# A shared feed-forward stage by Strassen block products, with the second projection after the fifth product

## The reference

```python
s1 = xf @ shared_fc1.T          # 3584 x 512 by 512 x 1408
s2 = xf @ shared_fc2.T          # the same shape
shared = jax.nn.silu(s1) * s2 @ shared_proj.T      # 1408 -> 512
y = y + jax.nn.sigmoid(xf @ shared_gate_w.T) * shared
```

## Time and profile before

| | |
|---|---|
| median of the timed runs | 1615.07 us |
| the profiled execution, its own time | 1618.94 us |
| its span, first to last instruction | 1617.2 us |
| mean granted clock of TensorE | 0.99 |
| busy: PE, DVE, ACT, POOL | 97%, 54%, 39%, 35% |
| shared stage, first to last matmul | 1050.0 to 1609.7 us |
| busy in it: PE, DVE, ACT, POOL | 556.8, 185.8, 105.5, 56.3 us |

### The profile page before, as it was taken

The page is one execution under the profiler, slowest core; times in us unless marked ns, Lnnn a source line. Parts: engine busy times, 40 slices in busy tenths (PEclk is TensorE's granted clock), DMA queues, the critical chain, the costliest instruction groups (busy, mean ns, idle before and its releaser), DMA issues.

```text
span 1617.2 us, 32041 instructions
## 1 busy us (share of the span) xinstructions
PE 1563.1 (97%) x11388; PEld 1333.0 (82%) x11388; DVE 871.8 (54%) x1685; ACT 632.7 (39%) x1970; POOL 559.7 (35%) x507
## 2 busy tenths in 40 slices
PE   4999999999889999999999999999999999999998
PEld 3788888888768799999999999888788888888886
DVE  4567777766655576666666666544423233232322
ACT  3877777877743333332333333332111111121211
POOL 4233446445442355555555555220200100000010
PEclk9899999999999999999999999999999999999999
DMA  4233355443466366666566666454401203030110
GB/s 156 64 103 97 79 103 90 95 86 76 89 140 162 108 257 244 243 228 245 221 246 222 245 235 242 154 208 145 147 28 47 78 8 104 26 104 26 56 49 26
DMA packets 85684, 213.53 MB, mean 132 GB/s; under 512 B 38208, under 2 KB 39232, under 8 KB 80864
## 3 DMA queue, kind: packets, MB, share of 16 engines
q1 hardware_dynamic: 73424, 179.20, 35.3%
q0 software_dynamic: 12176, 33.20, 6.1%
HBM read 163.35 MB, written 49.02 MB: 131 GB/s over the span
## 4 chain that ended last, share of the span: by engine, by line
PE 86%; issue 4%; DVE 3%; POOL 3%; ACT 2%; DMA 2%; DVEq 0%; POOLq 0%; SPq 0%; ACTq 0%
PE psum L665 54%; PE psum L972 11%; PE psum L917 9%; PE psum L763 2%; PE psum L888 2%; PE psum L754 2%; PE psum L782 1%; ACT probs L1071 1%; PE psum L791 1%; PE psum L850 1%; PE psum L814 1%; POOL xn L1275 1%; PE psum L771 1%; PE psum L678 1%; POOL lists_dram L1241 1%
## 5 line engine op out<-in xcount | busy, mean ns | idle before, releaser
L665 PE MATMUL psum<-gT_hi,wj_hi 128*128 128x256 f32 (+1 forms) x840 | 238.9, 284 | 0.0
L665 PE MATMUL psum<-gT_lo,wj_hi 128*128 128x256 f32 (+1 forms) x840 | 236.4, 281 | 0.0
L665 PE MATMUL psum<-gT_hi,wj_lo 128*128 128x256 f32 (+1 forms) x840 | 235.7, 281 | 0.0
L1350 POOL DMA_INDIRECT routed<-expert_out_dram,slot_b x56 | 56.3, 1006 | 489.2 <-DVE slot_b L1737 336.5
L665 PE MATMUL psum<-nT_hi,ws_hi 128*128 128x512 f32 x528 | 209.8, 397 | 6.4 <-DVE nT_lo L1689 6.4
L1755 DVE TENSOR_TENSOR h_s<-psum,silu_s 128x512 f32<-128x512 f32 x66 | 45.6, 692 | 308.1 <-PE psum L665 308.1
L665 PE MATMUL psum<-nT_hi,ws_lo 128*128 128x512 f32 x528 | 211.0, 400 | 0.0
L665 PE MATMUL psum<-nT_lo,ws_hi 128*128 128x512 f32 x528 | 210.8, 399 | 0.0
L1312 POOL TENSOR_SCALAR wj_hi<-wj_raw 128x2816 fp32r<-128x2816 f32 x68 | 136.4, 2023 | 149.5 <-PE psum L917 123.2
L1071 ACT ACTIVATE probs<-psum,minus_max 112x112 f32<-112x112 f32 x512 | 176.3, 431 | 3.4 <-DVE minus_max L1437 3.4
L1679 DVE TENSOR_TENSOR wj_lo<-wj_raw,wj_hi 128x2816 fp32r<-128x2816 f32 x70 | 169.2, 2418 | 0.8 <-ACT wj_hi L1163 0.7
(11 more groups left out here) (219 smaller groups left out, 3581.8 us busy)
## 6 DMA issues: line engine op xcount, KB each, us to landing
wj_raw<-in_w_experts SPq DMA_DIRECT2D x35, 2176.0 KB, 8.6
expert_out_dram<-y_c SPq DMA_DIRECT2D x35, 512.0 KB, 2.7
wj_raw<-in_w_shared SPq DMA_DIRECT2D x22, 768.0 KB, 5.9
base<-x_dram SPq DMA_DIRECT2D x8, 1024.0 KB, 5.8
x_in<-in_x SPq DMA_DIRECT2D x32, 224.0 KB, 3.8
x_res<-in_x SPq DMA_DIRECT2D x32, 224.0 KB, 3.1
x_dram<-x SPq DMA_DIRECT2D x32, 224.0 KB, 2.8
normed_dram<-xn SPq DMA_DIRECT2D x32, 224.0 KB, 3.2
```

Source lines behind the costliest of these rows:

```text
L665: mm = pe.matmul(out_ap, u, v, start=(n == 0), stop=(n == last))
L1350: pool.indirect_dma_start(out=routed[:, b % 2, c, :], out_offset=None, in_=expert_out_dram, in_offset=bass.IndirectOffsetOnAxis(ap=slot_b[ ...
```

## The change

The 512 tokens of a group and the 512 input values are halved each, and so are pairs of chunks: a unit ("quads") is the first layer of two chunks for 512 tokens, as a product of 2 x 2 blocks. It is done with seven block products in place of eight (Strassen's scheme in Winograd's form). Each block product is 12 matmuls of 256 columns. Five units hold ten chunks; the eleventh ("one") stays as it was. The weights of a unit are loaded as four blocks, of which POOL makes seven (`sum_quads`, four additions or subtractions); a group's tokens are loaded as four blocks, and POOL makes four more (`sum_tokens`), so that there are eight, of which quads take seven. ACT and DVE split all of them into halves.

The halves of 5 units do not fit in SBUF. The stage now goes twice over the six groups: in the first run ("half 0") with units 0, 1, 2, in the second ("half 1") with unit 3, the single chunk, and unit 4. The first run stores its partial result back to `x1_dram`, the second adds to it. Weights of unit 3 and 4 are loaded, summed and split in the last group of the first run and the first of the second. Routed rows are added in the first run; those of the first 512 tokens in the second group of the second run.

What remains of a unit outside TensorE: the products land in banks 4 to 7, and DVE and ACT form the four result blocks (`m1`, `u2`, `u3`, `c22`, `c21`, `c12`) before SiLU, product and splitting. The two projections of a unit run in the unit behind it: one after its second product, the other after its fifth.

```diff
+        UNITS = ((("quads", 0, 0, (0, 1)), ("quads", 1, 1, (2, 3)), ("quads", 2, 2, (4, 5))),
+                 (("quads", 3, 0, (0, 1)), ("one", None, None, (6,)), ("quads", 4, 1, (2, 3))))
+        # weight block, token block, bank, fresh bank
+        PARTS = ((0, 0, 4, True), (5, 5, 5, True), (1, 2, 4, False), (2, 6, 6, True), (4, 4, 7, True), (3, 7, 5, True), (6, 3, 7, False))
...
 # PE
+            def part(half, g, i, q, n):
+                w, t, b, fresh = PARTS[n]
+                if i == 0 and n < 7:
+                    pe.wait_ge(S["t_split"], prepared_before(half, g) + PREPARED.index(t) + 1)
+                for f in range(2):
+                    for k in range(2):
...
+                        for m, (u, v) in enumerate(((a_hi, b_hi), (a_hi, b_lo), (a_lo, b_hi))):
+                            mm = pe.matmul(psum[:, b, f * HS:(f + 1) * HS], u, v, ...
+            def quads(half, g, i, q):
+                at_least(pe, S["sums_made"], summed(n - 1, "h11"))
+                part(half, g, i, q, 0)
+                at_least(pe, S["sums_made"], summed(n - 1, "c21"))
+                part(half, g, i, q, 1)
+                project_before(half, g, i, 0)
+                pe.wait_ge(S["copies_made"], copied(n, "m1"))
+                part(half, g, i, q, 2)
+                at_least(pe, S["sums_made"], summed(n - 1, "u3"))
+                part(half, g, i, q, 3)
+                at_least(pe, S["sums_made"], summed(n - 1, "c12"))
+                part(half, g, i, q, 4)
+                project_before(half, g, i, 1)
+                pe.wait_ge(S["sums_made"], summed(n, "u2"))
+                part(half, g, i, q, 5)
+                pe.wait_ge(S["sums_made"], summed(n, "c22"))
+                part(half, g, i, q, 6)
...
 # DVE, one unit
+                dve.tensor_tensor(m1[:, :, :], b5, m1[:, :, :], ALU.add).then_inc(S["sums_made"], 1)
...
+                if i == 2:
+                    low_behind(half, g, (0, 1))
+                    add_group(half, g, (1, 2))
...
+                dve.tensor_tensor(s1[:, 0, :], psum[:, 4, HS:ST], s1[:, 0, :], ALU.mult).then_inc(S["sums_made"], 1)
...
+                dve.tensor_tensor(u3[:, :, :], b6, m1[:, :, :], ALU.add).then_inc(S["sums_made"], 1)
+                if i == 2:
+                    low_behind(half, g, (2, 3))
+                if i == 1 and half == 0:
+                    place_group(half, g)
...
+                dve.tensor_tensor(c2[:, :, HS:ST], b7, u3[:, :, :], ALU.add).then_inc(S["sums_made"], 1)
+                before = unit_before(half, g, i) if i == 0 else None
+                if before:
+                    dve.wait_ge(S["proj_s_done"], chunks)
+                    for b in range(SB):
+                        add_shared(*before[0:2], b)
+                if i == 2:
+                    low_behind(half, g, (4,))
+                dve.wait_ge(S["part_done"], 7 * n + 6)
+                dve.tensor_tensor(c2[:, :, 0:HS], u3[:, :, :], b5, ALU.subtract).then_inc(S["sums_made"], 1)
+                dve.wait_ge(S["part_done"], 7 * n + 7)
+                dve.tensor_tensor(m1[:, :, :], b7, m1[:, :, :], ALU.add).then_inc(S["sums_made"], 1)
+                dve.wait_ge(S["copies_made"], copied(n, "c2"))
+                dve.tensor_tensor(c2[:, 0, :], c2[:, 0, :], c2[:, 1, :], ALU.mult).then_inc(S["sums_made"], 1)
+                dve.wait_ge(S["copies_made"], copied(n, "c12"))
+                dve.tensor_tensor(s1[:, 1, :], s1[:, 1, :], m1[:, 1, :], ALU.mult).then_inc(S["sums_made"], 1)
+                dve.wait_ge(S["hs_hi_made"], chunks + 1)
+                dve.tensor_tensor(hs_lo[:, 1, :], c2[:, 0, :], hs_hi[:, 1, :].bitcast(F32), ALU.subtract).then_inc(S["hs_split"], 1)
...
+                if i == 2:
+                    low_behind(half, g, (5, 6, 7))
+                    add_group(half, g, (3,))
+                if i == 1 - half:
+                    add_group(half, g, (0,))
...
 # POOL
+            def sum_quads(q):
+
+                w = quads_raw[UNITS_SLOT[q]]
+                pool.wait_ge(quads_loaded[q % 3], 64 * (q // 3 + 1))
+                for i, (to, a, b, op) in enumerate(((4, 2, 3, ALU.add), (5, 4, 0, ALU.subtract), (6, 1, 5, ALU.subtract), (2, 0, 2, ALU.subtract))):
...
+                    pool.tensor_tensor(w[:, to, :, :], w[:, a, :, :], w[:, b, :, :], op).then_inc(S["quads_summed"], 1)
...
+                if isinstance(n, int) and n == NJOBS - 2:
+                    sum_quads(0)
+                    sum_tokens(0, 1)
+                if last_job(n):
+                    sum_quads(1)
...
 # ACT, end of job 33
+                if isinstance(n, int) and n == NJOBS - 2:
+                    quads_high(0)
...
 # DVE, in the last job, behind chunk 0 and chunk 1
+                    elif i == 0:
+                        quads_low(0)
+                    else:
+                        for t in range(5):
+                            tokens_low(0, 1, t)
...
 # PE, at the very end
+            for j in range(SB):
+                y_of(1, 2, 0, j)
+                y_of(1, 2, 1, j).then_inc(S["y_block_done"], 1)
```

More of the change, by code:

```diff
@@ L108, in build_program @@
     WS = (2 * KC + 4) * P
+    HS = ST // 2
     ctx = ExitStack()
@@ new lines, in unit_before, with group_behind, quads_of @@
+        def unit_before(half, g, i):
+            if i:
+                return half, g, i - 1
+            if is_opening(g):
+                return (0, GB, 2) if half else None
+            return half, g - 1, 2
+        def group_behind(half, g):
+            return (1, 1) if is_turn(half, g) else (half, g + 1)
+        def quads_of(q):
+            return quads_hi[UNITS_SLOT[q]], quads_lo[UNITS_SLOT[q]]
+        UNITS_SLOT = (0, 1, 2, 0, 1)
+        PW_SEMS = (0, 1, 2, 0, 3, 1)
+        SUMS = ("u2", "h11", "u3", "c22", "c21", "c12", "h2", "h12")
@@ new lines, in chunk_of, with y_of @@
+            def chunk_of(half, i, n):
+                kind, _, _, places = UNITS[half][i]
+                return (1, places[0]) if kind == "one" else (1 - n, places[1 - n])
+            def y_of(half, i, n, j):
+                at, pw = chunk_of(half, i, n)
+                a_hi, a_lo = hs_hi[:, at, j * P:(j + 1) * P], hs_lo[:, at, j * P:(j + 1) * P]
+                last = i == 2 and n == 1
+                for m, (u, v) in enumerate(((a_hi, pw_hi[:, pw, :]), (a_hi, pw_lo[:, pw, :]), (a_lo, pw_hi[:, pw, :]))):
+                    mm = pe.matmul(bank(j), u, v, start=(i == 0 and n == 0 and m == 0), stop=(last and m == 2))
+                return mm
@@ L954, in hidden_s, with one @@
+            def one(half, g, i):
+                n = quads_before(half, g, i)
+                if is_opening(g):
+                    pe.wait_ge(S["one_split"], 1)
+                pe.wait_ge(S["t_split"], prepared_before(half, g) + 8)
+                for f, b in enumerate((4, 6)):
+                    pe.wait_ge(S["sums_made"], summed(n - 1, "u3" if f else "h11"))
                     pairs = []
                     for k in range(KC):
-                        cols = slice((c * KC + k) * P, (c * KC + k + 1) * P)
@@ new lines, in one @@
+            def one(half, g, i):
+                u = u3[:, :, :].rearrange("p f t -> p (f t)")
+                act.wait_ge(S["one_filled"], 2 * g - 1)
+                act.wait_ge(S["sums_made"], summed(quads_before(half, g, i) - 1, "c21"))
+                act.activation(u, bank(4), ACT.Silu).then_inc(S["one_silu"], 1)
+                act.wait_ge(S["one_made"], g)
+                act.wait_ge(S["proj_s_done"], chunks_before(half, g, i) - 1)
+                act.activation(hs_hi[:, 1, :], u, ACT.Copy).then_inc(S["hs_hi_made"], 1)
@@ L1188, in _, with shared_body @@
+            def shared_body(half, g):
+                for i, unit in enumerate(UNITS[half]):
+                    if unit[0] == "one":
+                        one(half, g, i)
+                    else:
+                        quads(half, g, i)
             act.wait_ge(S["phase_c_done"], 4)
@@ new lines, in add_routed, with place_group, add_group @@
+                    dve.wait_ge(S["routed_added"], 2 * (SB * n + b) + c + 1)
+            def place_group(half, g):
+                if half == 0:
+                    place_routed(g - 1, route_b, S["route_b_loaded"], 16 * base_turn(half, g))
+                elif isinstance(g, int) and g == 2:
+                    place_routed(GB, route_0, S["base_z_loaded"], 32)
+            def add_group(half, g, bs):
+                for b in bs:
+                    if half == 0:
+                        dve.wait_ge(S["base_loaded"], 16 * base_turn(half, g))
+                        add_routed(g - 1, b, base, route_b)
+                    elif isinstance(g, int) and g == 2:
+                        add_routed(GB, b, base_z, route_0)
```

547 lines of the change are left out of this document (378 added, 169 removed).

## The result

The changed kernel took 1628.43 us (median of five, 1625.90 to 1632.87) beside 1615.07 for the kernel before (five, 1613.65 to 1615.96): ratio 1.0091, interval [1.0076, 1.0106]. It is about 0.9% slower, as the forecast case said, but by 13 us and not by 3: inside the range of 1602 to 1632, above the 1611 to 1625 of the likeliest case. The profiled execution has a span of 1625.6 us, 8.4 more than before and 5.6 more than the sum of the prediction (1620). These two differences are too small by 3.1 us, for the changed kernel's execution was ahead when the changed part began.

A forecast was written before the change was run, and what follows sets the result against it. The prediction took PE issuing matmuls as the bound. Matmuls 515.9, waits 38.3, POOL 4 and clock 6 made 564 us; with start 1051.5 and tail 4.5 that is 1620, 1618 on the median's scale, range 1602 to 1632.

The forecast's parts named there:

- the forecast case: Whole kernel: the waits eat the gain, 3 us slower, 1611 to 1625 on the median's scale; chance 0.45.
- The gain: Shared stage: a unit's 84 matmuls at 0.119 us take 10.00 us against 11.22, saving 36.7 us over 30 units.
- wait of 0.3 us for `hs_lo` in each unit: Behind each unit's seventh product: chain of 3.07 us over a cover of 2.86, 0.31 us each, 9 us for 29 units.
- the first units: First unit of a group: adds of the group before delay the chain by 0.75 us; eleven such units, 8 us.
- the opening: Start of the shared stage: first unit waits 4.5 us for c22, the next about 2; 6.5 us together.
- POOL beside DVE in every group: POOL's sum_tokens stretch h2 and hs_lo by up to 1.3 us in eleven units, 0 to 14; 4 us taken.
- The clock: Opening, first unit, turn and end: four falls to 1.2 GHz of up to 1.9 us each; 6 us taken (2 to 9).
- The step that failed, opening: Job 34, ahead of the shared stage: it ends about 5 us later, so the stage starts at 1051.5 (1050 to 1053.5).
- The step that failed, turn: Third unit of group 6: late weights, then DVE work, put c22 at 49.5 to 50 against 47; 5 us (2 to 8).
- rival 4: The turn and the opening wait longer for weights, 8 us more, 1626; chance 0.07.
- Rival 3: POOL's sums fall on the chain in all groups, 14 us in place of 4, 1628; chance 0.12.
- rival 2: Shared stage: the waits are mostly covered, so the kernel is faster, 1603 on the median; chance 0.30.

The follow-up runs named there:

- the run of the turn alone: Changed kernel with GpSimd gathers, quads_hi, quads_lo and the block 2 add reordered in the third unit at the turn; ratio 1.0056 to the kernel before.
- the kernel with all of it together: Changed kernel with reordered opening and turn, adds of blocks 2 and 3 behind hs_lo, both projections early in each group's first unit; ratio 0.9932 to the kernel before.

## Why the prediction held and where it was off

**Right.** The gain: 256 columns at 0.119 us, so that the speed of the matmuls was never the question. The groups: 49.3 and 40.8 us forecast, 48.8 to 49.5 and 40.6 to 40.9 measured. The wait behind the first unit (1 us forecast; 0.54 to 0.80 and its restart), `c22` about 1 us late in the third (0.87 to 1.37 in groups 2 to 5), the end (3.8 and 3.6), the weights' landing at the turn 29 us into the group and their sums done at 35 (the group starts at 1305.3, since the projection at 1324.44 is 2.9 us into its second unit of 16.3; POOL sums from 1334.39 to 1340.3). The stage as a whole came out at 567.0 for 564, and the direction followed from the right cause, DVE's queue.

**Off by cancelling.** The "wait of 0.3 us for `hs_lo` in each unit" is there, and smaller. Where no other work is in the way, PE starts the projection 0.05 to 0.13 us late and its second matmul 0.1 late, 0.15 to 0.24 in place of 0.31: the chain runs over the cover of 2.86 by less than the 0.2 that I took. Behind the single chunk there is no wait. The sum with the first units (17 forecast, 15.6 measured) came near because a wait that I had not added up, for `hs_lo` at the turn (1.03), and short ones for `c22` in the second run stand in it too. In the first unit `c22` is 3.4 late and not 4.5 (the terms given for it add up to 12.2 and not to 12.5), and with the later units the opening comes out at 7.2 for 6.5. POOL beside DVE in every group is 0 where I took 4: `h2` and `hs_lo` there keep their 0.69. The clock cost 8.4 in the stage and some 1.2 in the last projection of job 34, for the 6 taken: besides the four falls that were forecast there is one behind the 1.93 us wait in the third unit of the first group, and the one at the turn holds for 26 matmuls behind the wait.

**The step that failed, opening:** "The stage starts at 1051.5 (1050 to 1053.5)". It started at 1055.3, and from the first matmul of job 34 the step is off by more: 25.3 us to the stage where 18.4 were forecast (1051.5 - 1033.1), the 3.1 us that this execution was ahead hiding the rest. The waits of job 34 are 10.0 in place of 5. The sums on POOL (1.29 each for 1.3), `quads_hi` (3.2) and `quads_lo` (3.88 for at most 4.3) were sized well. Wrong was "ACT and DVE five token blocks ahead of chunk 2, so the last projection waits 3 us more": 3 us is five blocks at 0.6 to 0.7, and four of them took 1.6 to 1.75 beside POOL's sums. I had the collision as a term, and put it into the groups, where it does not happen, and not into the job, where the loads of the second quad land at 1043.18 and release POOL's sums just as DVE comes to the `t_lo` (1043.47). With POOL held back the wait is 3.29, the 3 of the prediction.

**The step that failed, turn:** "the same 6.7 us of DVE work as above before `c22`: 49.5 to 50 ... 5 us". `c22` ended 57.9 us into the group. Up to the sums the step was exact; then the gathers were missing from it. They stand behind these sums in POOL's queue, so `quads_lo` ended at 46.4 us and not at 43, and the 6.7 us became 11.5, with a wait of 2.00 and the stretched add (2.03 for 0.75) and `t_lo` (1.75). The run with the add of block 2 moved took this wait to 4.50. So rival 4 came nearest in size (8 us more at turn and opening), but not for its reason: the weights were not late. Rival 3's 1628 is the measured median to 1 us, by luck: its collision in all groups is absent. Of the 10 us between 1618 and that median, 5.6 are in the span. The rest is the step from the span to the median: the forecast took 2 us off, as in the kernel before, whose profiled execution is 3.9 above its median; in the changed kernel, whose profiled execution is its median, the median is 2.8 above the span. Of rival 2, the faster one, the runs show what it would have needed: not covers that were there, but five changes in the order of the queues.

Open is why the changed kernel's runs spread over 7 us where those of before spread over 2.3. The fastest of them (1625.90) has the highest mean clock, 0.987 against 0.984 and 0.985, and falls behind waits of about 2 us, which come at some waits and not at others, would do it; that was not tried.

## What to carry to other kernels

When the bound engine gets less work, list for each of its remaining waits the whole queue of the engine that ends it, in order, with every queue that feeds that one: here two DVE instructions in each of six groups, moved behind later ones, took the ratio from 1.0091 to 1.0017, most of what the change had lost. Look at the places where loads, sums and splits happen once (opening, turn) by themselves; a sum over "the same work as above" misses what stands only there. Ask of each pair of VectorE and GpSimd instructions on SBUF whether they can run at the same time. And a late start that no view names is not one without a cause: look at the granted clock of its stretch and at what ended just before it.

## What the runs showed of the hardware

- DVE with two SBUF inputs beside a POOL sum of two SBUF inputs: 512 columns 0.69 to 1.6 to 1.78 us, 256 columns 0.42 to 1.80. With POOL moved away, 0.69 again.
- POOL's issue of an indirect gather takes 0.95 us; it took 4.50 in the changed kernel, 3.91 in the run of the turn alone and 3.90 in the kernel with all of it together, where it began 0.20, 0.80 and 0.81 us after a `quads_lo` (3.88, 3.89, 3.89), and each time it ended 0.82 us after that. That the one holds the other was not tried apart.
- A matmul that waits for a DVE result starts 0.05 to 0.13 us after it. The next one comes 0.1 us late, behind one that was 0.06 late as behind one that was 0.88 late: short waits that no view names made up 3.2 us of the stage.
- At a granted clock of 0.50, matmuls of 256 columns start 0.213 us apart, where they start 0.119 apart at 1.00.
- After a wait of 2.23 us the granted clock was 0.61 over 4.4 us in one group and 1.00 in another of the same kernel; no fall followed waits of 1.96 and 2.09 us in another run, and one followed a wait of 1.93 in the changed kernel.
